# Normalisations of the fp8 layer and of the banded attention, moved into the stages beside them

## What is computed

```python
x = x + _L0_attn_ref(_layernorm(x))          # gated slots, 16 heads
x = x + _L0_ffn_ref(_layernorm(x))           # fp8 linear
x = x + _L1_attn_ref(_layernorm(x))          # banded attention, 16 heads
x = x + _L1_ffn_ref(_layernorm(x))           # mixture of experts

def _layernorm(x, eps=1e-05):
    return (x - mean(x)) / sqrt(var(x) + eps)

def _L0_ffn_ref(x, weight, bias):
    amax_x, amax_w = max(abs(x)), max(abs(weight))        # over ALL tokens
    x_scale = amax_x / (448 * 0.8)
    w_scale = maximum(amax_x, amax_w) / (448 * 0.8)
    q = lambda t, s: (t / s).astype(float8_e4m3fn).astype(float32) * s
    return einsum('bsd,od->bso', q(x, x_scale), q(weight, w_scale)) + bias
```

## Time and profile before

| | us |
|---|---|
| median of three runs | 2098.75 |
| the profiled execution | 2093.93 |
| its span, first to last instruction | 2092.1 |
| end of the gated-slot stage (last bn_stats) | 922.7 |
| fp8 stage | 923.9 to 976.7 |
| normalising stage n1 | 977.5 to 994.5 |
| banded attention begins | 995.4 |

### The profile page before, as it was taken

How to read it: one execution, slowest core, us unless ns; L and a number is a source line. 1 busy time by engine, 2 the same in 40 slices (tenths; PEclk the granted TensorE clock), 3 DMA queues, 4 the chain that set the end, 5 groups by cost and what they waited for, 6 DMA issues and landing times. The chain is left out here.

```text
span 2092.1 us, 39447 instructions
## 1 busy us (share of the span) xinstructions
PE 1773.3 (85%) x14355; PEld 1494.5 (71%) x14355; DVE 1321.9 (63%) x2657; ACT 801.2 (38%) x1951; POOL 762.7 (36%) x1004
## 2 busy tenths in 40 slices
PE   5999999999999999944899999999985537488870
PEld 3888888888888888832688888888873426377760
DVE  5777787778777787768566666666655416233335
ACT  3444444444444444413355555555554002122220
POOL 3333433343334433343424234233212441255551
PEclk9999999999999999975899999999997659688885
DMA  2100010004900000001100001000005111645435
GB/s 90 46 0 0 1 46 0 0 0 147 235 0 0 2 0 0 0 8 65 41 2 22 21 2 42 2 2 1 1 1 199 64 71 40 175 132 145 149 108 219
DMA packets 72796, 108.87 MB, mean 52 GB/s; under 512 B 24988, under 2 KB 53852, under 8 KB 72028
## 3 DMA queue, kind: packets, MB, share of 16 engines
q1 hardware_dynamic: 62300, 77.51, 12.8%
q0 software_dynamic: 9216, 25.44, 3.4%
q10 hardware_dynamic: 1152, 4.19, 0.5%
HBM read 62.30 MB, written 45.09 MB: 51 GB/s over the span
## 5 line engine op out<-in xcount | busy, mean ns | idle before, releaser
L795 POOL TENSOR_TENSOR a_ms<-a_ms,a_esq 128x4 f32<-128x4 f32 x64 | 14.2, 222 | 447.5 <-DVE a_ms L710 447.5
L1867 POOL DMA_INDIRECT ys<-m_yb,m_dest x128 | 122.7, 958 | 141.2 <-ACT m_yb L1966 105.9
L1250 ACT ACTIVATE b_prob<-b_sc,b_nmax 128x128 f32<-128x128 f32 x256 | 99.7, 391 | 138.7 <-DVE b_nmax L1317 138.7
L1312 DVE SCALAR_TENSOR_TENSOR b_sc<-b_ps_s,window_mask 128x512 f32<-128x512 f32 x64 | 44.3, 692 | 135.6 <-PE b_ps_s L1154 135.6
L1130 PE MATMUL b_ps_u<-xh,b_w_hi 128*128 128x512 f32 x256 | 114.9, 449 | 3.9 <-DVE b_rope L1306 1.9
L596 DVE RECIPROCAL a_rz<-a_ps_sz 128x256 f32<-128x256 f32 x64 | 112.5, 1757 | 3.2 <-PE a_ps_sz L344 3.2
L1921 PE MATMUL m_ps_y<-m_wd,m_hT 64*128 x256 | 77.6, 453 | 37.5 <-ACT m_hT L1959 33.8
L684 DVE TENSOR_TENSOR a_mix_m<-a_ps_av,square_consts 128x512 f32<-128x512 f32 x64 | 44.3, 692 | 98.5 <-PE a_ps_av L430 98.5
L555 ACT ACTIVATE a_sq<-a_ps_og 128x512 f32<-128x512 f32 x64 | 38.2, 597 | 176.8 <-PE a_ps_og L450 161.4
L1385 POOL TENSOR_TENSOR b_Q<-b_rope 128x512 f32<-128x512 f32 x32 | 41.4, 1294 | 168.1 <-DVE b_rope L1306 168.1
L1130 PE MATMUL b_ps_u<-xl,b_w_hi 128*128 128x512 f32 x256 | 102.5, 401 | 0.0
(11 more groups left out here) (335 smaller groups left out, 6082.1 us busy)
## 6 DMA issues: line engine op xcount, KB each, us to landing
xs<-a_zeros SPq DMA_DIRECT2D x32, 528.0 KB, 14.9
m_xb<-xs SPq DMA_DIRECT2D x32, 528.0 KB
wgu_all<-wgu SPq DMA_DIRECT2D x4, 2048.0 KB, 14.2
b_w_raw<-Wb SPq DMA_DIRECT2D x12, 512.0 KB, 5.3
m_wd<-wd SPq DMA_DIRECT2D x2, 2048.0 KB, 17.9
f_got<-ys SPq DMA_DIRECT2D x8, 512.0 KB, 15.7
f_got<-ys ACTq DMA_DIRECT2D x8, 512.0 KB, 14.9
X<-x SPq DMA_DIRECT2D x2, 1024.0 KB, 7.4
```

The source lines that it names most:

```text
L1250: last = nc.scalar.activation(prob[:, n % 2, h, :], sc[:, h % 2, h // 2, :], ACT.Exp, bias=nmax[:, at:at + 1], accum_out=den[:, n % 2, 0, ...
L1867: pool.indirect_dma_start(ys, bass.IndirectOffsetOnAxis(ap=dest[:, i % HOMES, j:j + 1], axis=0), yb[:, i % RING, j // 2, j % 2, :], None). ...
```

## The change

It does four things.

1. **Gated-slot stage, last head group.** Six tiles (normalised x, mean and variance, rstd, maxima, weight, bias) are allocated around this stage and handed to the fp8 stage. Behind each bn_stats VectorE makes the tile's mean and variance; one step later GpSimd makes its rstd (two instructions, behind its `chunk` copies) and VectorE normalises it and takes its maximum (`norm_out`, behind `o_low`). The last two tiles follow after the last step. VectorE's and GpSimd's loops over this group's middle steps are written out. SP loads weight and bias here, behind its stores to `xs`.
2. **fp8 stage.** Loads, means, rstd, normalisation and the large maximum are gone; two small maxima remain. `partition_all_reduce` gives way to a TensorE turn of the 128 x 2 maxima, a maximum over the 2 x 128, a copy that spreads it, and a second turn. The bias adds wait for nothing.
3. **Stage n1 is gone.** The banded attention normalises, turns and splits x itself, in pairs of tiles: pairs 0 to 2 ahead of the first unit, pair 3 behind unit 2, pairs 4 to 7 in steps 0 to 3. The turns borrow the banks `ps_m` and `ps_y`.
4. **First weights of the banded attention.** They arrive in three parts with a semaphore each (part, cos, sin, part, part, mask, output weights); ScalarE makes all high parts, GpSimd all low parts (`low`, `low_v`) ahead of its first `combine`; `project_v(0)` moves ahead of unit 4.

The core of the diff:

```diff
@@ abc_stage, vector
-                    measure_tile(nc, X, stats, tile)
+                    measure_tile(nc, X, stats, tile).then_inc(c["out_stat"], 1)
+                    dve.wait_ge(c["out_stat"], done(G - LAST))
+                    nc.vector.bn_aggr(out_meanvar[:, ds(tile, 1), :].rearrange("p a b -> p (a b)"),
+                                      stats[:, ds(tile, 1), :]).then_inc(c["out_aggr"], 1)
+            def norm_out(G, tile):
+                dve.wait_ge(c["out_pow"], done(G - LAST))
+                nc.vector.tensor_scalar(out_n[:, ds(tile, 1), :], X[:, ds(tile, 1), :],
+                                        out_meanvar[:, ds(tile, 1), 0:1].rearrange("p a b -> p (a b)"),
+                                        out_rstd[:, 1, ds(tile, 1)], ALU.subtract, ALU.mult)\
+                    .then_inc(c["out_norm"], 1)
+                dve.wait_ge(c["out_norm"], done(G - LAST))
+                nc.vector.tensor_reduce(out_amax[:, ds(tile, 1)], out_n[:, ds(tile, 1), :], AX, ALU.max,
+                                        apply_absolute_value=True)
...
                 if prev:
                     o_low(H - 1, n)
+                if final and tile_two is not None:
+                    norm_out(H - 2, tile_two)
...
             y_add(NG * STEPS - 1, 2 * CH - 1, True)
+            norm_out(NG * STEPS - 2, CH - 1)
+            norm_out(NG * STEPS - 1, 2 * CH - 1)
@@ abc_stage, gpsimd
+            def rstd_out(G, tile):
+                pool.wait_ge(c["out_aggr"], done(G - LAST))
+                hold(pool, held)
+                nc.gpsimd.tensor_scalar(out_rstd[:, 0, ds(tile, 1)],
+                                        out_meanvar[:, ds(tile, 1), 1:2].rearrange("p a b -> p (a b)"), EPS, None,
+                                        ALU.add).then_inc(c["out_eps"], 1)
+                pool.wait_ge(c["out_eps"], done(G - LAST))
+                nc.gpsimd.tensor_tensor(out_rstd[:, 1, ds(tile, 1)], out_rstd[:, 0, ds(tile, 1)], minus_half[:, 0:1],
+                                        ALU.pow).then_inc(c["out_pow"], 1)
...
                     chunk(H + 2, b, tile_after_next)
+                if tile_two is not None:
+                    rstd_out(H - 2, tile_two)
@@ fp8_stage, gpsimd
-            rstd_of(nc, pool, meanvar, rstd, minus_half, aggr, rs, eps_added, held)
-            pool.wait_ge(bias_in, 16)
             with pool.Fori(0, NT) as t:
                 xt = X[:, ds(t, 1), :].rearrange("p a d -> p (a d)")
-                pool.wait_ge(normed, t + 1)
                 nc.gpsimd.tensor_tensor(xt, xt, bias[:], ALU.add).then_inc(biased, 1)
-            pool.wait_ge(maxed, 1)
-            nc.gpsimd.partition_all_reduce(amax_all[:], amax[:], P, bass.bass_isa.ReduceOp.max).then_inc(reduced, 1)
@@ fp8_stage, vector
-            aggregate(nc, stats, meanvar, aggr)
...
-            linked(nc.vector.tensor_reduce(amaxes[:, 0:B], xn[:].rearrange("p (b j) d -> p b (j d)", b=B), AX, ALU.max,
-                                           apply_absolute_value=True))
-            nc.vector.tensor_reduce(amax[:, 0:1], amaxes[:, 0:B], AX, ALU.max)
+            nc.vector.tensor_reduce(amax[:, 0:1], amaxes[:, 0:NT], AX, ALU.max)
             nc.vector.tensor_reduce(amax[:, 1:2], amaxes[:], AX, ALU.max).then_inc(maxed, 1)
+            dve.wait_ge(p_max, 1)
+            linked(nc.vector.tensor_reduce(peak[:], psM[:], AX, ALU.max))
+            nc.vector.tensor_copy(peak_all[:], peak[:].broadcast_to([2, P])).then_inc(peaked, 1)
+            dve.wait_ge(p_all, 1)
+            linked(nc.vector.tensor_scalar(scale[:], psA[:, 0:2], 1.0 / QMAX, None, ALU.mult))
@@ fp8_stage, tensor
+            pe.wait_ge(maxed, 1)
+            nc.tensor.transpose(psM[:], amax[:], ident).then_inc(p_max, 1)
+            pe.wait_ge(peaked, 1)
+            nc.tensor.transpose(psA[:, 0:2], peak_all[:], ident[0:2, 0:2]).then_inc(p_all, 1)
@@ window_stage, tensor
+            def turn_pair(i):
+                pe.wait_ge(normed, 2 * i + 2)
+                if i < EARLY_PAIRS:
+                    after(pe, x_lo, i - 2)
+                else:
+                    after(pe, x_lo, i - 1)
+                    after(pe, y_add, i - EARLY_PAIRS - 2)
+                for t in range(2):
+                    for k in range(KD):
+                        c = (k * 2 + t) * P
+                        last = nc.tensor.transpose(turned_in(i)[:, c:c + P], xn[:, i % 2, t, k * P:(k + 1) * P], ident)
+                last.then_inc(turned, 1)
...
+            turn_pair(0)
+            turn_pair(1)
+            turn_pair(2)
             for U in range(AHEAD):
+                if U == AHEAD - 1:
+                    project_v(0)
                 for c in range(2):
                     unit(U, c)
-            project_v(0)
+                if U == 2:
+                    turn_pair(3)
...
+                if n + EARLY_PAIRS < NT // 2:
+                    turn_pair(n + EARLY_PAIRS)
@@ window_stage, scalar
+            x_high(0)
+            x_high(1)
+            high(0, 0)
+            high(1, 0)
+            x_high(2)
+            high(2, 0)
+            high(3, 0)
             high_v(0)
             high_wo(0)
+            x_high(3)
@@ window_stage, vector
+            for t in range(NT):
+                nc.vector.bn_aggr(meanvar[:, t, :], stats[:, t, :]).then_inc(aggr, 1)
+            normalise(0)
+            normalise(1)
+            x_low(0)
+            normalise(2)
+            x_low(1)
+            x_low(2)
+            for U in range(AHEAD):
                 rotate(U, 0)
                 rotate(U, 1)
+                if U == 0:
+                    normalise(3)
+                if U == 3:
+                    x_low(3)
@@ window_stage, gpsimd
+            root(0)
+            root(1)
             nc.gpsimd.memset(K[:, 0, :, :, 0:WIN], 0.0).then_inc(zeroed, 1)
             nc.gpsimd.memset(Vs[0:WIN, 0, :], 0.0).then_inc(zeroed, 1)
+            low(0, 0)
+            low(1, 0)
+            low(2, 0)
+            low(3, 0)
+            root(2)
+            root(3)
+            low_v(0)
             pool.wait_ge(zeroed, 2)
             for U in range(AHEAD):
                 combine(U)
@@ program
-                norm_stage(nc, "n1", X, stats, ident, xh, xl, preload=(preload_window, 16 * 7),
-                           split=[w[:, :, 0:2 * UW] for w in (w_raw, w_hi, w_lo)])
```

More of the change, by code:

```diff
@@ L1095, in window_stage, with turned_in, pair_cols @@
                              "o_lo", "y_add"))
-        block = ctx.enter_context(nc.Block())
+        first_in = [sem(f"first_in{i}") for i in range(3)]
+        cos_in, sin_in, mask_in, first_wo = (sem(n) for n in ("cos_in", "sin_in", "mask_in", "first_wo"))
+        const, aggr, eps_added, rs, normed, turned, x_hi, x_lo, held = (
+            sem(n) for n in ("const", "aggr", "eps_added", "rs", "normed", "turned", "x_hi", "x_lo", "held"))
+        EARLY_PAIRS = 4
+        block = ctx.enter_context(nc.Block())
+        c2 = lambda ap: ap.rearrange("p (k x) -> p k x", k=KD)
+        def turned_in(i):
+            return ps_m if i < EARLY_PAIRS and i % 2 == 0 else ps_y
+        def pair_cols(i):
+            return slice(2 * i * P, 2 * (i + 1) * P)
         c3 = lambda ap: ap.rearrange("p (h x) -> p h x", h=GH)
@@ L1116, in _ @@
                     sp.wait_ge(low, g)
-                window_weights(sp, w_raw, wo_raw, w_in, wo_in, A, g)
+                for part in range(3):
+                    window_weights(sp, w_raw, part, w_in, A, g)
+                window_out_weights(sp, wo_raw, wo_in, A, g)
         @block.tensor
@@ L1265, in o_high, with x_high @@
                 nc.scalar.copy(oT_hi[:], c3(ps_m[:])).then_inc(o_hi, 1)
-            for u in range(2):
-                act.sem_inc(w_high[u], 1)
-            for u in range(2, UNITS):
-                high(u, 0)
+            def x_high(i):
+                act.wait_ge(turned, i + 1)
+                nc.scalar.copy(xh[:, :, pair_cols(i)], c2(turned_in(i)[:])).then_inc(x_hi, 1)
+            x_high(0)
[5 more added lines that the diff above has]
+            high(3, 0)
             high_v(0)
             high_wo(0)
+            x_high(3)
             act.wait_ge(zeroed, 2)
@@ L1293, in _, with normalise, x_low @@
         def _(dve):
-            def low(u):
-                cols = slice(u * UW, (u + 1) * UW)
-                dve.wait_ge(w_high[u], 1)
-                nc.vector.tensor_tensor(w_lo[:, :, cols], w_raw[:, :, cols], w_hi[:, :, cols].bitcast(F32),
-                                        ALU.subtract).then_inc(w_low[u], 1)
+            def normalise(i):
+                for t in (2 * i, 2 * i + 1):
+                    dve.wait_ge(rs, t // 4 + 1)
+                    if t >= 4:
+                        dve.wait_ge(turned, i - 1)
+                    nc.vector.tensor_scalar(xn[:, i % 2, t % 2, :], X[:, t, :], meanvar[:, t, 0:1], rstd[:, 1, t:t + 1],
+                                            ALU.subtract, ALU.mult).then_inc(normed, 1)
+            def x_low(i):
```

(20 more changed lines are left out.)

171 lines of the change are left out of this document (93 added, 78 removed).

## The result

The changed kernel took 2072.66 us (median of four runs, 2066.29 to 2077.16) beside 2101.02 for the kernel before on the same chip (four runs): ratio 0.986, 95% interval 0.9831 to 0.989. The forecast was 2077.9, range 2067 to 2090. Two later comparisons, with six runs of the changed kernel each, gave 0.9909 (0.9892 to 0.9926) and 0.9915 (0.9892 to 0.9938), that is 17.1 and 15.4 us instead of 28.4. So the time is explained from the profile, stretch by stretch, and not from one median.

The account below looks back on a forecast made before the run. TensorE was taken to bound last head group and attention, with a 98.5 us seam of waits between. Fp8 stage with tail -12.7, attention -8.7, last group +0.5: -20.9 from 2098.75 gives 2077.9 us, range 2067 to 2090.

Parts of the forecast that it names:

- Steps 0 to 3: Banded attention's first steps: four pair turns cost +2.0 us, normalisations beside `combine` and shared-bank waits +2.0 (0 to 4).
- Last head group and tail: Gated-slot stage: added VectorE and GpSimd work costs the group +0.5 us (0 to 2), the bare tail +2.5.
- Scale 3.6 us into the stage: fp8 stage: small maxima, two turns and a copy give the scale at 930.0, 17.7 us earlier.
- Adds next: fp8 stage: GpSimd's 16 bias adds become late, VectorE pushing them back 2.9 us to 941.3, ahead of the first subtraction.
- short ones pass between: fp8 stage: short VectorE instructions slip between GpSimd's adds, read from adds of 0.72 us each with normalisations among them.
- the strict lock of the first rival: fp8 stage: ports lock both ways, first L894 at 946.3, fp8 part -7.8 us, total 2082.8 us; 20%.
- Stage and tail: fp8 stage together with the last head group's tail: -12.7 us, bounds -15.8 and -7.8.
- Start of the attention: From the start of the stage behind fp8 (T): first scores at T + 31 instead of T + 43.7, -12.7 us.
- The sum: Whole kernel: -12.7 - 8.7 + 0.5 = -20.9 us, giving 2077.9 us.
- The start bound by blocked normalisations: Attention's start: GpSimd's queue and held-back normalisations bind, scores at T + 35, 4 us in steps, total 2083.9 us; 14%.
- The stretched group: Last head group's 14 steps lengthen; 1.5 us a step eats the saving; 6% no change, 3% slower.
- a scale that stays late: fp8 stage: TensorE's two hops cost what the all_reduce did (4.6 us), only 2 us; no chance given.

Follow-up runs that it names:

- moved bias adds: Changed kernel with 14 of the 16 bias adds moved from the fp8 stage into GpSimd's queue in the last head group; 2074.12 us, ratio 0.9868.
- The attention's part alone: Gated-slot and fp8 stages as in the kernel before, n1 gone and banded attention as changed; 2098.31 us, ratio 0.9982.

## Steps 0 to 3: where the forecast was too good

TensorE of the changed kernel, all its waits from the first scores on:

```profile
1000.45 0.66 PE L1268 MATMUL b_ps_y<-square_consts,b_xn 128*128 128x128 f32 x4 [2.28 <-DVE b_xn L1395]
...
1010.77 0.66 PE L1268 MATMUL b_ps_y<-square_consts,b_xn 128*128 128x128 f32 x4 [0.83 <-DVE b_xn L1395]
...
1022.18 0.63 PE L1268 MATMUL b_ps_y<-square_consts,b_xn 128*128 128x128 f32 x4 [1.85 <-DVE X L1444]
...
1033.40 0.63 PE L1268 MATMUL b_ps_y<-square_consts,b_xn 128*128 128x128 f32 x4 [1.83 <-DVE X L1444]
```

Each of the four turns of a pair is late. The four themselves cost 0.46 to 0.50 us, 1.9 together, as forecast (2.0). The waits cost 6.8, where the forecast allowed 2.0 (0 to 4). The rest is TensorE's clock in step 0. The two parts of that step, up to the first wait and from there on, in the changed kernel and in the one with moved bias adds:

```profile
995.25:1000.25 5.00, 2.92 (x12) 2.04 (x12) 3.25 (x7) 2.35 (x10) 3.81 (x3) 1.00 0.00 1
1000.25:1005.58 5.33, 5.13 (x48) 3.93 (x50) 2.04 (x5) 2.44 (x5) 2.76 (x3) 0.68 1.00 343
...
988.91:993.91 5.00, 2.92 (x12) 2.04 (x12) 3.25 (x7) 2.35 (x10) 3.80 (x3) 1.00 0.02 1
993.91:997.70 3.79, 3.59 (x48) 2.88 (x50) 2.03 (x5) 2.13 (x4) 2.38 (x3) 1.00 0.94 325
```

Both waited the same 2.28 us, then one had a granted clock of 0.68 for the 48 matmuls that follow and the other kept 1.00: 1.5 us. The attention's part alone kept 1.00 too (8.79 us for the step). What decides it is not shown. So 1.9 + 6.8 + 1.5 accounts for 10.2 of the 10.6 us.

The waits have two causes. In steps 0 and 1 the normalisation stands in VectorE's queue behind the reciprocal of this step's softmax, which waits for ScalarE, and behind two tables; TensorE has nothing else to do then, as the turn stands ahead of the turn of the probabilities in its queue. In steps 2 and 3 the pair is normalised in time (1020.38), but the bank `ps_y` still holds the last projection until its add into X (L1444, 1021.62), two instructions further down.

### Normalised one step earlier

```diff
@@ window_stage, vector
+            normalise(4)
...
-                if n + EARLY_PAIRS < NT // 2:
-                    normalise(n + EARLY_PAIRS)
+                if n + EARLY_PAIRS + 1 < NT // 2:
+                    normalise(n + EARLY_PAIRS + 1)
```

> The changed kernel with pairs 4 to 7 each normalised one step earlier on VectorE, nothing else. If steps 0 and 1 are long by TensorE's wait for the normalisation (2.3 and 0.8 us and the low clock behind it), they become 7 to 8.5 and 9.3 us; steps 2 and 3, which wait for the add into X on the shared bank, stay at 11.2. If it is one cause, all four shorten alike.

One execution, 2083.83 us. TensorE's waits in steps 1 to 3:

```profile
1011.38 0.39 PE L1254 MATMUL b_ps_y<-b_wo_hi,b_oT_hi 128*128 128x256 f32 x1 [1.22 <-DVE xl L1400]
...
1020.39 0.63 PE L1268 MATMUL b_ps_y<-square_consts,b_xn 128*128 128x128 f32 x4 [1.85 <-DVE X L1444]
...
1030.94 0.63 PE L1268 MATMUL b_ps_y<-square_consts,b_xn 128*128 128x128 f32 x4 [1.18 <-DVE X L1444]
```

Step 0 fell from 10.33 to 6.84 us, so its wait was the normalisation's, and the low clock behind the wait went with it. Step 1 stayed at 10.37 where 9.3 was expected: the turn came in time, but `out_project` now waits for the same bank, until `x_low` has read the pair out of it. Steps 2 and 3 still wait for the add into X (11.20 us as before, and 10.57). The bank is a cause of its own.

### Two more pairs ahead of the first step

```diff
-        EARLY_PAIRS = 4
+        EARLY_PAIRS = 6
...
-                if U == 2:
-                    turn_pair(3)
+                if U >= 2:
+                    turn_pair(U + 1)
```

with `normalise`, `x_high` and `x_low` of pairs 4 and 5 put behind units 2 to 4, and pairs 6 and 7 normalised a step early.

> The changed kernel with six pairs ahead of the first scores (pairs 3, 4, 5 behind units 2, 3, 4, each in a hole of TensorE), pairs 6 and 7 in steps 0 and 1, normalised one step early. If steps 0 to 3 are long because TensorE waits there for normalisations (2.3 and 0.8 us) and for the bank, held until the add into X (1.85 and 1.83 us), those waits go: steps 0 and 1 at some 9.3 us, 2 and 3 at 8.7, first scores not over 2 us later, and the kernel is 5 to 8 us under the changed one. If the length is the turns themselves or the steps' own filling, it only shifts: within 2 us of the changed one.

2081.52 us (five runs), ratio 0.9882 (0.9864 to 0.9901), 2.9 us below the changed kernel on the same chip, where 5 to 8 were expected; by the two profiles of that chip the fifth product is 6.6 earlier (107.3 from the fp8 stage's start, against 113.9). A normalisation beside `combine`, and what is left of TensorE's waits in the steps:

```profile
992.20 2.29 DVE L1397 TENSOR_SCALAR b_xn<-X,b_meanvar,b_rstd 128x256 f32<-128x256 f32 x2
...
1002.74 0.66 PE L1223 MATMUL b_ps_t<-square_consts,b_prob 128*128 128x128 f32 x4 [1.12 <-ACT b_prob L1336]
...
1013.38 0.39 PE L1254 MATMUL b_ps_y<-b_wo_hi,b_oT_hi 128*128 128x256 f32 x1 [0.57 <-DVE xl L1402]
```

The waits of 6.8 us become 1.7; steps 0 to 3 last 6.83, 9.73, 8.71 and 8.75. The price is 2.5 us ahead of the first product (T + 33.1): more pairs, whose normalisations take 1.7 to 2.3 us instead of 0.73 while GpSimd combines.

### Both repairs

> The bias adds moved and six pairs ahead of the first scores. The two act in different stages, so the savings add: 7 and 6.5 us from the last bn_stats to the fifth scores under the changed kernel, some 101 us from the fp8 stage's start to the fifth scores' evacuation against 114. Timed, 30 us under before, 13 under the changed kernel. If the one takes the other's room (a pair's loads of the weights become late when the stage comes earlier), less than 10.

> Bias adds moved and six pairs early, once more beside the changed kernel. By the seam (99.75 us against 114) it is 14 us under the changed kernel; the runs so far have 2071.9 against 2084.4, on different chips.

The bias adds and the pairs moved together: 2071.92 us (six runs), ratio 0.9855 (0.9828 to 0.9883); and again, beside the third run of the changed kernel on one chip, 2074.16 against 2086.98, 12.8 less (14 expected), ratio to the kernel before 0.9871 (0.9852 to 0.9889). The fifth product comes 99.8 and 99.6 us after the fp8 stage's start. By the profile the two repairs nearly add (-9.5 and -6.9 alone, -14.5 and -14.6 together, all against the 114.2 of the first profile); of the 1.9 us missing, 1.5 are the low clock of step 0, which is absent from the profile of each. On top of the adds the pairs bring 5.0 us by the profile, but only 2.2 by the medians, and the intervals of the two overlap. This version beats both kernels.

## Why the prediction was right, and where it was not

- **Last head group and tail**: right, +0.7 and +2.2 for +0.5 and +2.5. The power of one column took 0.58 us, between the two rows that bounded it.
- **Scale 3.6 us into the stage**: right (3.34). The two turns and the copy stand for an all_reduce that came 5.74 us late.
- **Adds next**: the mechanism was right, and the moved adds show it. The size was off: they ended 16.6 us into the stage, 14.9 were foreseen. The step that failed is "up to the first L894 VectorE has eight such instructions". At the measured 0.28 us that slips between, those eight (5.33 us alone) push by 3.1, close to the 2.9 put down for them; but while the adds went on VectorE didn't stop there, and the three of the second `add_magic` (2.61 us alone) pushed by another 1.8. The reading that "short ones pass between" was also too kind: the adds came every 0.73 us in the kernel before, but each normalisation among them took 0.81 instead of 0.41; and L936, read as ending when L894 had, ended 0.56 us behind it (956.82 and 956.26). On the other side the strict lock of the first rival (946.3, 19.9 us into the stage) was not reached, because an add held VectorE up for 0.44 of its 0.72 us only. Stage and tail gave -11.2 for -12.7.
- **Start of the attention**: right to 1.5 us at every milestone. Without the 1 us that was added for a low clock the forecast would have been T + 30 for T + 29.7, although the clock was at 0.68 in the first 15 us; another 0.9 came from scores at the full clock, since the fall is counted from T to the end of the scores.
- **Steps 0 to 3**: the mis-sized term, +10.6 for +4.0. The prediction said that "normalisations that must pass beside `combine` and waits of `out_project` on the shared bank" cost 2.0 (0 to 4). Normalisations in these steps were never held back by the port (0.73 for two). What it left out is their place in VectorE's queue, behind the softmax, and that the bank binds in both directions: the turn waits for the add into X as well. The waits are 6.8 us. A fall of the clock behind the first wait, 1.5 us, was not in the forecast.
- **The sum**: -20.9 forecast, -14.8 by the profile, and -15.4, -17.1 and -28.4 by the three comparisons. The median of the first lies 5.2 us below the forecast although the seam gave 6 less than foreseen. The two errors have opposite signs: of the 28.4 us of that comparison the seam explains 14.8, and 13.6 are from outside it, 5.1 of them seen in the profiles, in untouched code. That the first median lies as near to 2077.9 as it does is luck; with the seam's saving alone it would be about 2084, as in the later comparisons. The first four executions of the changed kernel were some 12 us faster than the later ones and had a higher mean granted clock (0.918 against 0.913 and 0.914); what raised it stays open.
- **Rivals**: the lock both ways occurred in a weaker form, 1.7 us of the 5 foreseen. The start bound by blocked normalisations occurred in one profile of three of the changed kernel, and its longer steps 0 to 3 occurred for another reason. The stretched group, and a scale that stays late, did not occur.

## What to carry to other kernels

Work put into a stage that one engine bounds must be costed by its place in the queues: ask, for every added wait of the bounding engine, what stands ahead of the instruction that it waits for, and for every borrowed buffer who holds it from the other side. Where a long filler was hidden behind a wait, removing the wait makes the filler the bound, so look for its next home at once: here the adds were worth another 7.7 us in a stage where GpSimd had room. Before a median is explained, compare a stretch of unchanged code in the two profiles; here it moved by as much as the change did, and with the granted clock. A merged row hides what happens to each instruction in it, so look at the single durations before taking two engines to pass each other freely.

## What the runs showed of the hardware beyond that

- A VectorE instruction beside a run of GpSimd adds (128 x 256, two SBUF inputs) takes its own time and 0.40 to 0.43 us more (0.52 in one of eleven), whatever its length (0.48, 0.69 and 1.23 alone; 0.41 in the kernel before), and the two engines alternate one by one. Beside longer GpSimd instructions it waits for the whole rest (3.82 us for 0.73 behind `low_v`; 2.71 for 0.69 beside the 2.72 us subtraction in the run with moved adds).
- A run of 48 writes of zeros held up a copy of 2 x 128 for 11.06 us, and another run of 24 gave way to scalings (0.85 us instead of 0.31 for the four zeros beside them).
- A power on GpSimd takes 0.58 us for one column (the median of sixteen, up to 0.93) where it takes 1.04 for four.
- TensorE waited 2.28 or 2.29 us in step 0 of the banded attention in seven profiles; in five the granted clock was 0.68 behind the wait, in two it stayed at 1.00.
